# A two-expert mixture layer: every expert on every token, or each expert on its own gathered tokens

## The chip, the core and the metric

The kernel runs on one core of a Trainium2 chip. The metric is the device time of one execution in microseconds (us). The engines are PE (matrix multiply; PEld is its weight load), DVE (vector), ACT (activation), POOL (GpSimd) and SP, which here only issues DMAs. PSUM is the memory that PE writes; it has eight banks of 128 x 512 floats.

## The reference, cut to what matters

x has 4096 tokens (2 x 2048) of 256 features. The same mixture-of-experts layer (MoE) runs twice, before and after a full attention; an LSTM layer, a causal attention and a second LSTM follow, and the change touches none of them.

```
x = x + 0.5 * ffn(layernorm(x))
x = x + attention(layernorm(x))
x = x + 0.5 * ffn(layernorm(x))
...
def ffn(x):
    probs = sigmoid(xt @ gate_w.T + gate_b)          # 6 experts
    w, idx = top_k(probs, 2)
    w = w / (sum(w) + 1e-08)
    ge = sum(one_hot(idx, 6) * w[..., None])         # 0 but for two experts of a token
    for e in range(6):
        h = silu(xt @ ew1[e].T) * (xt @ ew3[e].T)
        y = y + ge[:, e:e + 1] * (h @ ew2[e].T)
    z = silu(xt @ fc1.T) * (xt @ fc2.T) @ fc3.T      # shared expert, every token
    return y + z
```

All matrices are 256 x 256. A token has weight 0 for four of its six experts.

## The kernel before, in words

x stays in SBUF as `k.X` (128 partitions x 32 tiles of 128 tokens). `program` runs the stages one after another; between two stages all engines meet. `moe_stage` is the first and the third stage.

It works on 8 blocks of 512 tokens (`NBLK`), and in each block on 7 experts: the six and the shared one. Every product of floats is split in a high and a low part (`x_hi`, `x_lo`, `w_hi`, `w_lo`), and three products stand for one, so the first layer of one expert on one block (`up`) is 2 halves of 12 matmuls with 512 columns, and the second layer (`down`) is 24 matmuls with 256 columns. An **expert block** below is one `up` and one `down`. There are 8 x 7 = 56 of them in a stage.

All seven experts' split weights stay in SBUF; they are split once, in the first block (`split`, ACT at L377 and DVE at L484).

For each half of `up`, ACT takes the sigmoid (L395), DVE multiplies twice (L449, L453), ACT rounds the result to the high part (L387) and POOL makes the low part (`blockwise` of POOL, L274). `down` waits for it. DVE then adds the block's output, times the token's weight for that expert, into x (`update`, L465).

The routing of block n+1 is put between the experts of block n: DVE's layer norm (L107 to L120, L133, with one POOL step at L126), PE's transposes (L142), ACT's and DVE's split of x (L363, L473), PE's gate (L292, eight matmuls of 512 columns), a sigmoid, a transpose back (L299), and DVE's choice of two experts (`gate`, L422 to L441). The order on each engine is the order in which the code is written, and semaphores tie the engines together. SP loads weights only. POOL issues no DMA in this stage; it issues some in the causal attention (L1606, L1615).

## Time and profile before

| | us |
|---|---|
| median of 3 runs | 4684.81 (4669.04 to 4697.14) |
| the profiled execution | 4671.09 |
| its span, first to last instruction | 4669.5 |
| PE busy in it | 4239.2 (91%) |
| DVE busy | 3004.6 (64%) |
| ACT busy | 2295.4 (49%) |
| POOL busy | 682.8 (15%) |

A busy PE is one that has a matmul in flight; matmuls overlap, so the mean duration of one is longer than the distance between two starts. The two MoE stages lie at about 16 to 542 us and 2178 to 2699 us.

### The profile page before, as it was taken

The numbers are of one execution on the slowest core, as the hardware profiler recorded it, in microseconds if no ns is written. First come the engines' busy times: TensorE is split into PE (matmuls) and PEld (weight loads), VectorE is DVE, ScalarE is ACT, GpSimd is POOL, SyncE is SP. The second block draws the span as 40 slices with busy tenths as digits, with TensorE's granted clock in tenths as the row PEclk, the third lists the DMA queues.
The fourth block names the chain that finished last, engine by engine and source line by source line (L and its number), as shares of the span: only waits on it lengthen the run. The fifth ranks groups of instructions, "written<-read, shape, count | busy, mean of one in ns | idle before, by whom it ended". The sixth has DMA issues, their size and how long they took to land. (4 is left out here: it accounts for less than half of the span.)

```text
span 4669.5 us, 79371 instructions
## 1 busy us (share of the span) xinstructions
PE 4239.2 (91%) x25648; PEld 2522.6 (54%) x25648; DVE 3004.6 (64%) x5513; ACT 2295.4 (49%) x4375; POOL 682.8 (15%) x698
## 2 busy tenths in 40 slices
PE   7999969999999999986999989639999999997688
PEld 6888743333333333324888855525656656654454
DVE  5556668888888888835656533746666666663432
ACT  3222317777777777761332222214656556655222
POOL 2232200000000000000233200532222222220000
PEclk9999979999999999987999999868999989998789
DMA  2000172323323322203000000476667667662401
GB/s 85 0 0 0 52 146 38 46 34 43 46 34 44 46 38 39 32 6 120 8 0 0 1 20 0 150 198 179 188 176 184 188 165 186 191 158 52 131 20 36
DMA packets 173944, 359.15 MB, mean 77 GB/s; under 512 B 40586, under 2 KB 104714, under 8 KB 156810
## 3 DMA queue, kind: packets, MB, share of 16 engines
q1 hardware_dynamic: 154634, 304.20, 28.5%
q0 software_dynamic: 18944, 50.35, 3.9%
q8 instruction: 196, 3.21, 0.3%
q14 instruction: 170, 1.39, 0.1%
HBM read 209.71 MB, written 152.06 MB: 77 GB/s over the span
## 5 line engine op out<-in xcount | busy, mean ns | idle before, releaser
L1314 DVE TENSOR_REDUCE full_tops<-psum 128x1 f32<-128x1024 f32 x1024 | 1206.2, 1218 | 184.0 <-PE psum L1218 184.0
L1271 ACT ACTIVATE full_probs<-psum 128x512 f32<-128x512 f32 x2048 | 1065.8, 602 | 299.2 <-PE psum L1190 295.1
L1781 ACT ACTIVATE causal_probs<-psum 128x512 f32<-128x512 f32 (+3 forms) x1280 | 640.2, 533 | 397.9 <-PE psum L1653 230.0
L1190 PE MATMUL psum<-full_q,full_k 49*128 49x512 f32 x2048 | 653.3, 475 | 23.2 <-ACT full_probs L1271 17.2
L1832 DVE TENSOR_REDUCE causal_tops<-psum 128x1 f32<-128x1024 f32 (+7 forms) x704 | 586.8, 857 | 112.6 <-PE psum L1704 112.6
L1190 PEld LDWEIGHTS psum<-full_q,full_k 49*128 49x128 f32 x2048 | 284.5, 186 | 605.8 <-ACT full_probs L1271 576.9
L1199 PE MATMUL psum<-full_probs,full_vh 128*32 128x512 f32 x4096 | 556.8, 616 | 0.7 <-ACT full_probs L1271 0.7
L1218 PE MATMUL psum<-full_k,full_q 48*128 48x512 f32 x2048 | 402.0, 458 | 51.4 <-DMA full_k<-qk_split 23.6
L1653 PE MATMUL psum<-causal_q,causal_k 49*128 49x512 f32 (+3 forms) x1280 | 407.7, 451 | 14.2 <-ACT causal_probs L1781 8.3
L1704 PE MATMUL psum<-causal_k,causal_q 48*128 48x512 f32 (+4 forms) x1152 | 325.3, 414 | 70.2 <-DVE causal_tops L1847 33.4
L274 POOL TENSOR_TENSOR moe_h_lo<-moe_h,moe_h_hi 128x512 fp32r<-128x512 f32 x224 | 290.3, 1296 | 661.2 <-ACT moe_h_hi L387 661.2
L311 PE MATMUL psum<-moe_x_hi,moe_w_hi 128*128 128x512 f32 x896 | 351.9, 393 | 4.3 <-DVE moe_h L453 4.1
L311 PE MATMUL psum<-moe_x_lo,moe_w_hi 128*128 128x512 f32 x896 | 349.9, 391 | 0.0
L311 PE MATMUL psum<-moe_x_hi,moe_w_lo 128*128 128x512 f32 x896 | 348.8, 389 | 0.0
L1683 PE MATMUL psum<-causal_probs,causal_vh 128*32 128x384 f32 (+3 forms) x3712 | 343.0, 433 | 1.2 <-ACT causal_probs L1781 1.2
L449 DVE TENSOR_TENSOR moe_ts<-psum,moe_sg 128x512 f32<-128x512 f32 x224 | 154.7, 691 | 294.3 <-ACT moe_sg L395 294.1
L387 ACT CAST moe_h_hi<-moe_h 128x512 fp32r<-128x512 f32 x224 | 139.0, 620 | 384.7 <-DVE moe_h L453 384.7
L1606 POOL DMA_DIRECT2D band_scores<-xn x256 | 188.0, 734 | 841.8 <-DVE causal_tops L1847 838.1
L1218 PEld LDWEIGHTS psum<-full_k,full_q 48*128 48x128 f32 x2048 | 198.3, 190 | 207.5 <-DVE full_tops L1314 157.7
L1847 DVE CUSTOM_DVE_ANT_0 xn<-psum,causal_bias 128x160 f32<-128x160 f32 (+1 forms) x512 | 143.4, 317 | 202.0 <-issue 202.0
L395 ACT ACTIVATE moe_sg<-psum 128x512 f32<-128x512 f32 x224 | 133.9, 598 | 257.9 <-PE psum L311 256.6
L325 PE MATMUL psum<-moe_w_hi,moe_h_hi 128*128 128x256 f32 x896 | 255.9, 286 | 2.5 <-POOL moe_h_lo L274 2.5
(190 smaller groups left out, 6070.7 us busy)
## 6 DMA issues: line engine op xcount, KB each, us to landing
causal_bias<-bias_tiles SPq DMA_DIRECT2D x32, 1280.0 KB, 6.3
band_scores<-xn POOLq DMA_DIRECT2D x256, 160.0 KB, 4.2
full_q<-qk_split SPq DMA_DIRECT2D x192, 128.0 KB, 6.3
full_k<-qk_split SPq DMA_DIRECT2D x192, 128.0 KB, 7.1
causal_q<-rot_parts SPq DMA_DIRECT2D x192, 128.0 KB, 5.4
causal_k<-rot_parts SPq DMA_DIRECT2D x192, 128.0 KB, 6.4
bias_tiles<-causal_skew_rows SPq DMA_DIRECT2D x32, 640.5 KB, 3.4
bias_tiles<-causal_skew_rows SPq DMA_DIRECT2D x32, 640.0 KB, 3.3
```

The source lines that it names most:

```text
L274: nc.gpsimd.tensor_tensor(h_lo[:, r, u % C, :], hf[:, u % 2, :], h[:, r, u % C, :].bitcast(F32), ALU.subtract).then_inc(hl_ready, 1)
L311: last = nc.tensor.matmul(k.psum[:, 2 * (u % 2) + kind, :], W[wp][:, e, kind, c, m * P:(m + 1) * P], (xhi, xlo)[xp][:, half, c, :], start= ...
L1190: nc.tensor.matmul(k.psum[:, b, :], k_sb[at, q, kt * P:(kt + 1) * P], q_sb[at, q, n * BLK:(n + 1) * BLK], start=True, stop=True).then_inc( ...
L1199: last = nc.tensor.matmul(k.psum[32 * j:32 * j + VP, 7, :], vh[:, q % 2, kt, :], pT[:, kt % 4, j * BLK:(j + 1) * BLK], start=(kt == 0), st ...
L1218: last = nc.tensor.matmul(k.psum[:, b + c, :], q_sb[at, q, t * P:(t + 1) * P], k_sb[at, q, lo:lo + BLK], start=True, stop=True)
L1271: nc.scalar.activation(pT[:, kt % 4, n * BLK:(n + 1) * BLK], k.psum[:, bank(q, u), :], ACT.Exp).then_inc(p_ready, 1)
L1314: nc.vector.reduce_max(mx[:, q % 2, u // 2, u % 2:u % 2 + 1], src, AX_X).then_inc(m_free, 1)
L1653: last = nc.tensor.matmul(k.psum[:, b, 0:(hi - lo) * P], k_sb[at, q, kt * P:(kt + 1) * P], q_sb[at, q, lo * P:hi * P], start=True, stop=no ...
L1683: last = nc.tensor.matmul(k.psum[32 * j:32 * j + VP, 7, tiles[0] // QB * P:BLK], vh[:, q % 2, kt, :], pT[:, n % 2, first:first + QB * (len ...
L1704: last = nc.tensor.matmul(k.psum[:, b + side, at0:at0 + hi - lo], q_sb[at, q, t * P:(t + 1) * P], k_sb[at, q, lo:hi], start=True, stop=True)
L1781: nc.scalar.activation(dst, k.psum[:, bank(q, u), 0:(hi - lo) * P], ACT.Exp).then_inc(p_ready, 1)
L1832: last = nc.vector.reduce_max(mx[:, r, t, entry:entry + 1], both[:, off:off + hi - lo], AX_X)
```

## The change

`moe_stage` is rewritten; a token now meets the shared expert and its two experts only. In four phases:

1. **Shared expert with the routing.** For each of 8 blocks the shared expert runs (8 expert blocks), and the routing goes on: `choose` and `weigh` as before, then `positions` on PE (six small matmuls with a triangle and with ones) counts for each token and expert how many tokens came before it, `locate` on DVE turns that into a slot number in a list of its expert, and POOL writes the token's number to the two slots with indirect DMAs of 128 x 4 bytes (`scatter`, 8 a block, 64 in all). SP stores the normalised rows to DRAM (`XN`).
2. **Plan.** `schedule` on DVE works out which expert each of 21 blocks belongs to and where its list lies.
3. **21 expert blocks** of 512 list places each. SP loads the block's token numbers, POOL gathers the rows with four indirect DMAs of 128 rows of 1 KB (`gather`), PE transposes them, ACT and DVE split x and also the weights of the block's expert (`split`, `rest`, in a ring of three), `up` and `down` run as before, ACT copies the output (`out`) and SP stores it. 8192 pairs of token and expert fill at least 16 blocks, and six lists round up to at most 21; 21 are always run.
4. **Combine.** After all stores, POOL gathers for each of the 32 tiles of x its two output rows (64 indirect DMAs of 128 x 1 KB), and DVE adds them with their weights.

So there are 8 + 21 = 29 expert blocks in a stage in place of 56. The code is written out, without loops. The heart of the diff:

```diff
-                looped(pool, NBLK, blockwise)
+                def scatter(n):
+                    pool.wait_ge(idx_ready, n + 1)
+                    for t in range(n * TB, (n + 1) * TB):
+                        for s in range(2):
+                            pool.indirect_dma_start(
+                                out=k.TOKENS[:, :], out_offset=bass.IndirectOffsetOnAxis(ap=idx[:, s, t:t + 1], axis=0),
+                                in_=token[:, t:t + 1], in_offset=None).then_inc(k.scattered, 16)
+                def gather(b):
+                    v = NBLK + b
+                    pool.wait_ge(s_id[b % 4], 16 * (b // 4 + 1))
+                    pool.wait_ge(t_ready, 2 * (v - 2) + 2)
...
+                    for t in range(TB):
+                        pool.indirect_dma_start(
+                            out=k.xn[:, v % 2, t, :], out_offset=None, in_=k.XN[:, :],
+                            in_offset=bass.IndirectOffsetOnAxis(ap=idr[:, b % 4, t:t + 1], axis=0)).then_inc(k.gathered[v % 2], 16)
...
+                for v in range(NBLK - 2):
+                    rest(v + 1, 0)
+                    rest(v + 1, 1)
+                    scatter(v + 2)
+                    if v + 4 < NBLK:
+                        ln.pool_rstd(pool, v + 4, v % 2)
...
+                for v in range(NBLK, NV - 1):
+                    rest(v + 1, 0)
+                    if v + 3 < NV:
+                        gather(v + 3 - NBLK)
+                    rest(v + 1, 1)
+                for r in range(2):
+                    pool.wait_ge(s_y[r], 16 * ((NX + 1 - r) // 2))
+                pool.wait_ge(back_ready, 1)
+                for g in range(TT):
+                    if g >= 8:
+                        pool.wait_ge(c_done, g - 7)
+                    for s, ring in enumerate((k.xn, ybuf)):
+                        pool.indirect_dma_start(
+                            out=ring[:, g % 8 // TB, g % TB, :], out_offset=None, in_=k.YS[:, :],
+                            in_offset=bass.IndirectOffsetOnAxis(ap=back[:, s, g:g + 1], axis=0)).then_inc(k.back[g % 8], 16)
```

PE, phases 1 and 3 (`up(v, m)` is one half, `down(v, pair)` too):

```diff
-                    for e in range(E + 1):
-                        if e < E:
-                            up(n, half, e + 1)
...
-                        down(n, half, e)
+                transpose(0)
+                gate(0)
+                positions(0)
+                transpose(1)
+                gate(1)
+                positions(1)
+                up(0, 0)
+                up(0, 1)
+                for v in range(NBLK - 2):
+                    transpose(v + 2)
+                    up(v + 1, 0)
+                    gate(v + 2)
+                    up(v + 1, 1)
+                    down(v, 0)
+                    positions(v + 2)
+                    down(v, 1)
...
+                transpose(NBLK)
+                transpose(NBLK + 1)
+                up(NBLK, 0)
+                up(NBLK, 1)
+                for v in range(NBLK, NV):
+                    if v + 1 < NV:
+                        up(v + 1, 0)
+                    if v + 2 < NV:
+                        transpose(v + 2)
+                    if v + 1 < NV:
+                        up(v + 1, 1)
+                    down(v, 0)
+                    down(v, 1)
```

The new gate has the tokens as the stationary side, so its result needs no transpose back: for each of four tiles one matmul for the bias and four for x, of six columns each. ACT and DVE:

```diff
+            # ACT, phase 3
+                for v in range(NBLK, NV):
+                    if v + 1 < NV:
+                        hidden(v + 1, 0)
+                    if v + 2 < NV:
+                        upper_x(v + 2)
+                    if v + 1 < NV:
+                        hidden(v + 1, 1)
+                    out(v - NBLK, 0)
+                    out(v - NBLK, 1)
+                    if v + 3 < NV:
+                        split(v + 3 - NBLK)
+            # DVE, phase 1
+                for v in range(NBLK - 2):
+                    lower_x(v + 2)
+                    hidden(v + 1, 0)
+                    choose(v + 2)
+                    hidden(v + 1, 1)
+                    weigh(v + 2)
+                    update(v)
+                    locate(v + 2)
+                    if v + 3 < NBLK:
+                        apply(v + 3)
+                    if v + 4 < NBLK:
+                        ln.dve_stats(dve, v + 4, v % 2, (v + 4) * TB)
+            # DVE, phase 4
+                for g in range(TT):
+                    dve.wait_ge(k.back[g % 8], brought(g))
+                    xt = k.X[:, g, :]
+                    nc.vector.scalar_tensor_tensor(xt, k.xn[:, g % 8 // TB, g % TB, :], wgt[:, 0, g:g + 1], xt,
+                                                   ALU.mult, ALU.add).then_inc(c_half, 1)
+                    dve.wait_ge(c_half, g + 1)
+                    nc.vector.scalar_tensor_tensor(xt, ybuf[:, g % 8 // TB, g % TB, :], wgt[:, 1, g:g + 1], xt,
+                                                   ALU.mult, ALU.add).then_inc(c_done, 1)
```

`hidden(v, m)` is the sigmoid, the two products and the rounding of one half; `rest(v, m)` on POOL is the old L274; `split` and `rest` of the weights read the block's expert from the plan with a register load first.

**POOL in the loop over the 21 blocks.** Before, POOL's queue in a MoE stage held the low part of each half and the layer norm's step:

```order
L265 MEMSET moe_pT 128x1024
L126 ISA
L126 TENSOR_TENSOR lnv<-lnv,neghalf 128x4
L149 UNCONDITIONAL_BRANCH
L149 ISA
L274 TENSOR_TENSOR moe_h_lo<-moe_h,moe_h_hi 128x512
```

Now, around the change from phase 1 to phase 3 (`normed` is `XN`, `slot_tokens` the lists):

```order
L376 DMA slot_tokens<-moe_token,moe_idx 24576x1 x8
L395 TENSOR_TENSOR moe_h_lo<-moe_h,moe_h_hi 128x512 x2
L388 DMA xn<-normed,moe_ids 128x256 x8
L395 TENSOR_TENSOR moe_h_lo<-moe_h,moe_h_hi 128x512
L388 DMA xn<-normed,moe_ids 128x256 x4
L395 TENSOR_TENSOR moe_h_lo<-moe_h,moe_h_hi 128x512 x2
L388 DMA xn<-normed,moe_ids 128x256 x4
```

A block's four gathers stand between the low parts of two halves, and the gather of a block stands behind the low part of the block two before it.

**DVE at the end of an iteration of phase 1**, with its waits: what stands behind the wait for `down` (the update, L758), up to the rows that the next transposes need (L133):

```order
L758 SCALAR_TENSOR_TENSOR X<-psum,X 128x512 [waits moe0_dn_ready] x2
L673 TENSOR_TENSOR moe_slot<-psum,moe_tables 128x24 [waits moe0_pos_ready]
L676 TENSOR_TENSOR moe_slot<-moe_slot,moe_sel 128x24 [waits moe0_pos_free]
L678 TENSOR_REDUCE moe_hi_slot<-moe_slot 128x4 [waits moe0_l_dve]
L679 TENSOR_REDUCE moe_both<-moe_slot 128x4
L681 TENSOR_TENSOR moe_lo_slot<-moe_both,moe_hi_slot 128x4 [waits moe0_l_dve]
...
L693 TENSOR_REDUCE moe_wgt<-moe_top_w 128x4 [waits moe0_wgt_ready]
L694 TENSOR_REDUCE moe_wgt<-moe_is_low 128x4
L133 TENSOR_SCALAR xn<-X,lnv 128x256 [waits moe0_ln_rstd,moe0_xn_stored1,moe0_t_ready]
L133 TENSOR_SCALAR xn<-X,lnv 128x256 x3
```

Before, the layer norm of the next block stood among the experts of a block, five expert blocks ahead of the `up` that reads it; now it stands behind the wait for the last `down` of the iteration, and PE's next instruction after that `down` is the transpose that needs it.

## Rows read from the trace of the kernel before

**Rows 1.** The page: busy tenths of PE in 40 slices of the span.

```profile
PE   7999969999999999986999989639999999997688
```

**Rows 2.** Windows: PE, PEld, DVE, ACT, POOL busy (count), clock, DMA share, GB/s.

```profile
110.00:170.00 60.00, 60.00 (x337) 50.41 (x336) 35.50 (x70) 18.70 (x32) 18.32 (x15) 1.00 0.01 1
```

**Rows 3.** Timeline of PE, start and duration in us: one expert block.

```profile
290.43 0.28 PE L325 MATMUL psum<-moe_w_hi,moe_h_hi 128*128 128x256 f32 x1
...
293.30 0.40 PE L311 MATMUL psum<-moe_x_hi,moe_w_hi 128*128 128x512 f32 x1
...
298.77 0.28 PE L325 MATMUL psum<-moe_w_hi,moe_h_hi 128*128 128x256 f32 x1
```

**Rows 4.** Timeline: the first MoE stage's start, its first up, its end.

```profile
16.21 0.95 POOL L265 MEMSET moe_pT<- 128x1024 f32 x1 [15.51 <-POOLq L49]
...
32.87 0.47 PE L311 MATMUL psum<-moe_x_hi,moe_w_hi 128*128 128x512 f32 x1
...
541.54 0.76 DVE L465 SCALAR_TENSOR_TENSOR X<-psum,X 128x256 f32<-128x256 f32 x2 [0.68 <-PE psum L325]
```

**Rows 5.** The two lines whose DMAs POOL issues: min/median/max ns, landing.

```profile
L1606 POOL DMA_DIRECT2D band_scores<-xn x256: 725/725/902, 3121.7 to 4248.0; - x128
...
DMA to landing us min/median/max: 2.3/4.2/11.7
...
L1615 POOL DMA_DIRECT2D band_compact<-band_scores x32: 1117/1136/1145, 3169.3 to 4251.2; - x32
...
DMA to landing us min/median/max: 4.2/5.4/10.6
```

**Rows 6.** Groups by shape, 37 to 542 us: busy us, mean ns, idle before.

```profile
L274 POOL TENSOR_TENSOR moe_h_lo<-moe_h,moe_h_hi 128x512 fp32r<-128x512 f32 x112 | 145.2, 1296 | 330.6 <-ACT moe_h_hi L387 330.6
...
L449 DVE TENSOR_TENSOR moe_ts<-psum,moe_sg 128x512 f32<-128x512 f32 x112 | 77.3, 690 | 147.0 <-ACT moe_sg L395 146.8
L387 ACT CAST moe_h_hi<-moe_h 128x512 fp32r<-128x512 f32 x112 | 69.5, 621 | 194.3 <-DVE moe_h L453 194.3
...
L465 DVE SCALAR_TENSOR_TENSOR X<-psum,moe_ge,X 128x256 f32 x96 | 40.8, 475 | 18.2 <-PE psum L325 18.0
...
L473 DVE TENSOR_TENSOR moe_x_lo<-psum,moe_x_hi 128x512 fp32r<-128x512 f32 x14 | 8.9, 679 | 0.0
...
L377 ACT CAST moe_w_hi<-moe_w_in 128x1536 fp32r<-128x1536 f32 x4 | 5.9, 1482 | 0.0
```

**Rows 7.** The split of the weights on DVE: min/median/max ns.

```profile
L484 DVE TENSOR_TENSOR moe_w_lo<-moe_w_in,moe_w_hi x14: 1742/1759/2174, 26.5 to 2236.2; 128x1536 fp32r<-128x1536 f32 x14
```

**Rows 8.** Timeline of DVE: layer norm, and the first and last routing operation.

```profile
16.62 1.41 DVE L107 BATCH_NORM_STATS2 st<-X 128x6 f32<-128x256 f32 x4 [15.49 <-PEq L49]
...
20.05 1.38 DVE L133 TENSOR_SCALAR xn<-X,lnv 128x256 f32<-128x256 f32 x4 [1.13 <-POOL lnv L126]
...
33.43 0.31 DVE L422 TENSOR_TENSOR moe_gt<-moe_pr 128x144 f32<-128x144 f32 x1 [5.19 <-ACT moe_pr L367]
...
35.86 0.18 DVE L441 SCALAR_TENSOR_TENSOR moe_ge<-moe_wsel,moe_tot 128x24 f32<-128x24 f32 x1
```

**Rows 9.** Timeline of PE: transposes and small products.

```profile
21.54 1.94 PE L142 MATMUL psum<-ident_sb,xn 128*128 128x128 f32 x8 [21.54 <-DVE xn L133]
...
94.22 0.60 PE L299 MATMUL psum<-ident_sb,moe_pT 128*128 128x128 f32 x4
...
2708.03 5.28 PE L2311 MATMUL psum<-big,arena 128*128 128x1 f32 x24 [9.65 <-DMA big<-in_bo]
```

**Rows 10.** DMA issues: count, KB each, median us to landing.

```profile
qk_split<-qkvf_parts SPq DMA_DIRECT2D x32, 512.0 KB, 4.2
...
full_q<-full_rows SPq DMA_DIRECT2D x64, 8.0 KB, 1.9
```

**Rows 11.** Windows at the start of the second MoE stage, columns as above.

```profile
2182.00:2193.00 11.00, 8.45 (x20) 2.87 (x21) 3.32 (x4) 4.51 (x5) 0.00 (x0) 0.60 0.47 172
2193.00:2197.00 4.00, 4.00 (x21) 3.33 (x20) 3.14 (x11) 3.43 (x4) 0.00 (x0) 1.00 0.01 4
```

More of the change, by code:

```diff
@@ new lines, in moe_stage @@
+        more = sb("more", [P, E, NBLK])
+        nblk = sb("nblk", [P, E])
+        prior = sb("prior", [P, E, E])
+        first = sb("first", [P, E])
+        total = sb("total", [P, 1])
+        past = sb("past", [P, NX, E - 1])
+        base = sb("base", [P, NX, E - 1])
+        expert = sb("expert", [P, NX])
+        valid = sb("valid", [P, NX])
+        origin = sb("origin", [P, NX])
+        inner = sb("inner", [P, NX])
+        row = sb("row", [P, NX])
+        plan = sb("plan", [P, 2, NX], I32)
@@ new lines, in gate @@
+                def gate(n):
+                    pe.wait_ge(xl_ready, 2 * n + 2)
+                    for t in range(TB):
+                        out = k.psum[:, 6, t * E:(t + 1) * E]
+                        nc.tensor.matmul(out, one_row[:, :], gb[:, :], start=True, stop=False, skip_group_check=True)
+                        for x, half in enumerate((xhi, xlo)):
+                            for c in range(C):
+                                last = nc.tensor.matmul(out, half[:, n % 3, c, t * P:(t + 1) * P].bitcast(F32), gwT[:, c, :],
+                                                        start=False, stop=(x == 1 and c == C - 1), skip_group_check=True)
+                    last.then_inc(gate_ready, 1)
@@ new lines, in _ @@
+                up(NBLK - 1, 0)
+                up(NBLK - 1, 1)
+                for v in (NBLK - 2, NBLK - 1):
+                    down(v, 0)
[11 more added lines that the diff above has]
+                        up(v + 1, 1)
+                    down(v, 0)
+                    down(v, 1)
```

671 lines of the change are left out of this document (446 added, 225 removed).

## The prediction

> **What bounds the kernel now.** I read the page first. PE's busy line has two stretches of nines, slices 0 to 4 and 18 to 23 [rows 1]; these hold the two MoE stages. A window inside one shows PE busy for 60.00 of 60 us at the full granted clock (1.00, that is 2.4 GHz), while DVE has 35.5, ACT 18.7 and POOL 18.3 us [rows 2]. So PE sets the pace. The timeline gives its price: one `down` takes from 290.43 to 293.30, 2.87 us, and one `up` from there to 298.77, 5.47 us; an expert block is **8.34 us** [rows 3]. 56 of them are 467 of the 526 us of the stage, which runs from 16.2 to 542.3 us [rows 4]; the rest is start, transposes and gates. Nothing POOL does bounds this stage. The change takes away 27 expert blocks, 225 us of PE a stage, and puts in their place work that waits on POOL and on DMAs. I walk through the first stage on its own clock and take the same saving for the second.
>
> **Up to the first `up`.** Now it starts at 32.87 us [rows 4]. PE's new order has two whole routings ahead of it. Block 0's gate should end about where it does now, at 31.8. It is 20 small matmuls in place of 8 wide ones. The trace does not show this shape; the nearest rows are 24 products of one column in 5.28 us, 0.22 each, and 4 transposes in 0.60 us once PE is warm, about 0.12 each [rows 9]. So a gate costs 4.4 us cold and 2.4 warm, and 8 transposes 1.94 cold, 1.0 warm. DVE's small operations run at (36.04 - 33.43) / 10 = 0.26 us where each waits for the last [rows 8]; some of the new ones don't, so I take 0.23. `choose`, `weigh` and `locate` have 7 + 6 + 13 = 26 of them, 6.0 us. After 31.8: sigmoid and these 26, to 38; block 1's rows 1.4 and the next layer norm 2.7 [rows 8], to 42; low part of x 1.4 [rows 6], gate 4.4, choice and count 3. **First `up` at 51 us**, 18 later than now. A clock still at its low level there would cost up to 5 more: at the start of the second stage the granted clock is 0.60, about the 1.2 GHz level for most of the window, and 1.00 from 2193 on [rows 11].
>
> **Phase 1, six iterations.** PE has per block 8.34 + 1.0 + 2.4 + 0.7 = 12.4 us, but it waits. Followed round the loop from the transposes: DVE's layer norm 2.65, low part of x 1.36 [rows 6, 8], gate 2.4, half an `up` 2.7, sigmoid and two products 2.0, `weigh` 1.4; `down` is over by then; update 1.4, `locate` 2.9, normalised rows 1.4, and only then the next transposes. That is **18 us** an iteration, 5.5 of it PE idle behind `update`, `locate` and `apply`. The first ends at 76.5, since POOL puts 16 scatters ahead of its first low part; then four of 18, and 16.7 without the last `apply`: 165 us.
>
> **The price that decides: g**, POOL's time to issue one indirect DMA of 128 rows. The trace has none. Its two direct ones take 0.725 us and 1.136 us [rows 5]; the second has an irregular pattern. An indirect one must also fetch and use 128 separate numbers, so I take the dearer row, **g = 1.13**; below it the bound is 0.73, above it I allow 2.0, some 0.9 more than any row, since no row excludes it. Landing L after the issue: the shortest and the median landing of line L1606 are 2.3 and 4.2 us from the start of the issue [rows 5], so 1.6 to 3.5; I take 2.5, as SP's 512 KB stores run beside the gathers. The Trainium skill ("DMA: Bandwidth & Descriptors", Anatomy of one DMA) gives about 2.0 us and the bytes at 436 GB/s for a DMA from POOL; for 128 KB that is 2.3 us in all, an estimate of L = 1.2, by which the sum would be some 34 us lower over both stages. The trace's shortest landing agrees with it, its median does not.
>
> **From phase 1 to phase 3.** The last list numbers are ready at about 164.5. Then, in a row: 8 scatters 9.0, landing 2.5, a register load and the ids 3 (8 KB land in 1.9 [rows 10]), 8 gathers 9.0 because PE transposes two blocks before the first `up`, landing 2.5, transposes 1: **192 us**. The last two `down` and the plan (11 small operations, 2.8 us, and two splits) lie beside it.
>
> **Phase 3.** PE needs 1.0 + 8.34 = 9.34 us a block. ACT has 1.24 x 2 for the halves, 1.2 for x and 1.2 for the output (all at the 0.62 of the rounding), and 1.48 for the weights: 6.4. DVE has 2.8 + 1.36 + 1.76: 5.9 [rows 6, 7]. POOL has 2 x 1.3 + 4g = 7.1. None of these sums bounds. The chain does: from the end of the first half of one `up`: sigmoid, products and rounding 2.65, low part 1.3, four gathers 4.52, landing 2.5: 11.0 us, against 9.34 until PE reaches these transposes. A late transpose delays the next `up` but not the gather issued after the half before it, so only half of the difference is paid: a block takes 9.34 + (11.0 - 9.34) / 2 = **10.15 us**. The register loads on ACT and DVE have no row; hidden in the slack of both I take nothing, up to 10 us a stage. Sum: one `up` 5.5, 20 x 10.15, one `down` 2.9: 403 us. Copy and store 4.8 [rows 10]: **408 us**.
>
> **Combine.** All stores must land first, so nothing hides this. 64 x 1.13 = 72.3 us of issues; DVE needs 2 x 0.475 a tile [rows 6], less than two issues, so it follows. The last landing and two additions take 3.6: the stage ends at **484 us**, against 542.3. That saves **58 a stage, 116 in all**. The next stages start as now.
>
> **The sum** against the profiled execution: 4671.1 - 116 = 4555 us. That execution was 14 us below the median; against the median it is 4684.8 - 116 = **4569 us**.
>
> How it depends on g: entry to phase 3 has 16, phase 3 has 20 x 4 / 2 = 40 and the combine 64, so each us of g costs 120 us a stage. The gain of 58 is used up at **g = 1.61**.
>
> **Rivals.**
>
> *The issue is dear (the other side).* At g = 2.0 the entry grows 14 us, phase 1 about 10 (POOL then has 8 x 2.0 + 1 + 2.6 = 19.6 us a block, over the 18), phase 3 35 and the combine 56: 115 a stage, 4799 us. It decides from g = 1.61 on. For it: no row shows an indirect DMA, and this one has one number for each row, where a direct one has a stride. Against it: the irregular direct DMA costs only 0.4 more than the plain one. Chance 0.25.
>
> *The issue is cheap.* At g = 0.73 phase 3 falls to PE's 9.34 (16 less), the entry by 6, the combine by 26: 48 a stage, 4473 us. For it: 0.725 is by far the most frequent row. Against it: those DMAs have no list. Chance 0.12.
>
> *PE at the low clock in phase 1.* If waits of 5 us in every iteration keep the granted clock near 0.60 [rows 11], matmuls of 12.4 us take up to 10 more, seven times, and the start 5: up to 75 a stage, of which waits hide a third: 50. 4569 + 100 = 4669, no change. Against it: now the clock is 1.00 through the stage, though PE there never waits so regularly. Chance 0.08.
>
> *DVE and POOL in each other's way.* The split of weights reads two tiles in SBUF; it took 1.74 to 2.17 us [rows 7]. If each such operation holds POOL up whole, the combine has 64 x 0.475 = 30 and phase 3 has 21 x 1.76 / 2 = 18: 48 a stage, 4665 us, no change. The row's spread of 0.4 bounds what has been seen. The Trainium skill ("SBUF — State Buffer", Who interferes with whom) says that a DVE instruction with two SBUF inputs contends with a GpSimd instruction that reads SBUF; all of the combine's additions are such, and by that rule it would come out this way; no row settles whether a DMA issue counts as such an instruction. Chance 0.05.
>
> That the change does not do less work can be excluded: 29 expert blocks are written out, whatever the data.
>
> **Numbers.** Forecast 0.50, dear 0.25, cheap 0.12, clock 0.08, contention 0.05. A measurement of this kernel tells about 0.5%, 23 us, from no change; that is 0.1 in g. Forecast and cheap give faster, 0.62. Clock and contention count half as the same, and a slice of the dear case near g = 1.6 too: same 0.09. Dear, and the clock or contention on top of a somewhat dearer issue: slower 0.29. The range runs from the cheap case to the dear one, each cut slightly: 4480 to 4790.
>
> **What would show it.** In the profile after: POOL's DMA lines show g, best in the combine, where starts should be 1.13 apart and the stretch about 75 us long. The starts of the first halves in phase 3 should be 10.15 apart, with PE waiting for the gathers' DMAs. In phase 1 they should be 18 apart, with PE waiting for DVE's normalised rows, at clock 1.00. The first stage should end at 484 us, and the other stages should keep their lengths. The forecast is wrong if g is over 1.6, if 8.34 grows, or if another wait than the gather's sets phase 3.

## The result: 3.4% slower, where 2.5% faster was forecast

The changed kernel takes 4843.91 us (median, 4835.12 to 4853.72), the kernel before beside it 4690.98 (4669.04 to 4706.23). The ratio is **1.034**, 95% interval 1.030 to 1.038. The forecast was 4569 us, its range ended at 4790, and its break-even for g, POOL's price of an indirect DMA, was 1.61 us. The profiled execution took 4853.7 us, span 4852.2. The first stage ends at 619.2 us, against 542.3 before [rows 4] and 484 in the forecast; the second one is as much longer (77.6 us from its first transposes to its last addition). Twice 77 is 154; the difference of the medians is 153. Each stage missed its forecast by 135 us.

The page of the changed kernel, beside the slices shown of before [rows 1]:

```profile
PE   6868368999999999995878729666999999998688
...
PEclk8789687999999999976679859885999999999799
```

The nines of PE in the MoE stages (now slices 0 to 5 and 18 to 23) are gone, and the granted clock there is mostly 0.6 to 0.8. The windows of the first stage tell its parts apart:

```profile
core 0: us, PE busy (x) PEld busy (x) DVE busy (x) ACT busy (x) POOL busy (x), PEclk, DMA share, GB/s
...
80.00:110.00 30.00, 26.26 (x119) 23.09 (x120) 14.41 (x56) 3.99 (x8) 11.38 (x11) 0.67 0.08 18
...
140.00:180.00 40.00, 32.52 (x159) 28.89 (x158) 22.31 (x89) 6.18 (x11) 17.38 (x17) 0.71 0.13 27
...
220.00:275.00 55.00, 26.34 (x138) 23.62 (x137) 19.18 (x52) 10.31 (x13) 20.05 (x19) 0.70 0.20 20
...
330.00:500.00 170.00, 138.93 (x752) 120.40 (x751) 76.43 (x94) 77.36 (x122) 86.69 (x82) 0.91 0.28 87
...
540.00:620.00 80.00, 0.00 (x0) 0.00 (x0) 31.03 (x64) 0.00 (x0) 57.79 (x62) 0.50 0.35 102
```

Phase 1 (80 to 220) has PE busy for 0.8 to 0.9 of the time, but at a clock of about 0.7. The transition (220 to 275) has it busy for half. In phase 3 (330 to 500) it is busy for 82%. In the combine it does nothing for 80 us.

**The price g was right.** The source view of POOL's three indirect lines:

```profile
L376 POOL DMA_INDIRECT slot_tokens<-moe_token,moe_idx x128: 954/958/1896, 42.7 to 2490.5; - x128
```

```profile
L388 POOL DMA_INDIRECT xn<-normed,moe_ids x168: 942/946/1002, 256.0 to 2755.7; - x168
```

```profile
L432 POOL DMA_INDIRECT moe_y<-slot_outputs,moe_back x64: 942/946/948, 537.9 to 2864.6; - x64
```

0.946 us busy and 0.30 us between two make 1.25 from start to start; 1.13 was forecast. The combine ran from 536.6 to 619.2, 82.6 us where 75.9 was forecast. So neither rival about g holds, and the loss is elsewhere. That the number was near is in part luck: the forecast took the dearer row because 128 numbers must be fetched, and e6 below shows the same price for 64.

**Phase 1.** DVE's update of block v starts at 89.08, 115.98, 143.09, 170.30: **27.2 us** an iteration, where 18 was forecast. PE's timeline through a part of one:

```profile
148.42 1.97 PE L142 MATMUL psum<-ident_sb,xn 128*128 128x128 f32 x8 [3.74 <-DVE xn L133]
150.04 0.77 PE L484 MATMUL psum<-moe_x_hi,moe_w_hi 128*128 128x512 f32 x1
150.61 0.63 PE L484 MATMUL psum<-moe_x_lo,moe_w_hi 128*128 128x512 f32 x1
151.04 0.63 PE L484 MATMUL psum<-moe_x_hi,moe_w_lo 128*128 128x512 f32 x1
...
154.39 0.40 PE L484 MATMUL psum<-moe_x_lo,moe_w_hi 128*128 128x512 f32 x1
154.63 0.40 PE L484 MATMUL psum<-moe_x_hi,moe_w_lo 128*128 128x512 f32 x1
154.96 0.38 PE L454 MATMUL psum<-moe_gb,moe_one_row 1*128 1x6 f32 x2
155.27 0.61 PE L457 MATMUL psum<-moe_gwT,moe_x_hi 128*128 128x6 f32 x4
...
157.96 1.02 PE L457 MATMUL psum<-moe_gwT,moe_x_hi 128*128 128x6 f32 x4
...
162.01 0.77 PE L484 MATMUL psum<-moe_x_hi,moe_w_hi 128*128 128x512 f32 x1
...
167.92 0.31 PE L502 MATMUL psum<-moe_w_hi,moe_h_hi 128*128 128x256 f32 x1
```

The starts of the wide matmuls are 0.43 apart at 150.6 and 0.24 from 154.4 on, so the clock is at its low level (1.2 GHz) after the wait of 3.74 us, and comes back. It falls a second time inside the gate: four records of L457 take 0.61 at 155.27 and 1.02 at 157.96. It comes back only at 168. PE waits 3.74 us in an iteration, less than the 5.5 that were forecast, so its own work takes 23.5 us in place of 12.4. The gate itself is 40 records, two for each of 20 matmuls: 7.0 us here, 9.35 at the stage's start (26.3 to 35.6).

**The transition.** The timeline of all engines and of POOL, from the last scatter to the first gather:

```profile
236.88 1.76 DVE L768 TENSOR_TENSOR moe_w_lo<-moe_w_raw,moe_w_hi 128x1536 fp32r<-128x1536 f32 x1 [3.59 <-issue]
237.57 1.90 POOL L376 DMA_INDIRECT slot_tokens<-moe_token,moe_idx  x1 [0.30 <-issue]
...
254.05 3.73 SPq L350 DMA_DIRECT2D moe_ids<-slot_tokens  x4
...
255.98 1.00 POOL L388 DMA_INDIRECT xn<-normed,moe_ids  x1 [13.99 <-DMA moe_ids<-slot_tokens]
```

SP's load of the token numbers starts 16.5 us after the last scatter starts (12.3 in the second stage), where the forecast had 2.5 for the landing and 3 for register load and ids together.

**Phase 3** takes 12.4 us a block (the gathers' groups start at 304.18 and, 16 blocks later, at 502.69), where 10.15 was forecast. PE's waits from 262 to 530:

```profile
PE psum L142 <- DMA xn<-normed,moe_ids: 66.3, 13, 17.3
```

One of the 13 waits is the first, 17.3 us; the other twelve are 49 us, about 4.1 in every second block.

### The profile page after: what moved, and what is told of

Read it like the earlier page. It is cut to its first block and busy times, and to the rows that moved or that the text cites. A ratio compares the mean times of both kernels' runs of the same rounds, so it can differ in the third digit from the quotient of the medians.

```text
span 4852.2 us, 75781 instructions
## 1 busy us (share of the span) xinstructions
PE 4054.0 (84%) x24032; PEld 2387.4 (49%) x24032; DVE 2879.4 (59%) x5431; ACT 2283.3 (47%) x4341; POOL 942.0 (19%) x1014
## 5 line engine op out<-in xcount | busy, mean ns | idle before, releaser
L1526 PE MATMUL psum<-full_q,full_k 49*128 49x512 f32 x2048 | 661.5, 482 | 20.3 <-ACT full_probs L1607 13.4
L1535 PE MATMUL psum<-full_probs,full_vh 128*32 128x512 f32 x4096 | 567.0, 627 | 0.7 <-ACT full_probs L1607 0.7
L1989 PE MATMUL psum<-causal_q,causal_k 49*128 49x512 f32 (+3 forms) x1280 | 412.0, 456 | 14.6 <-ACT causal_probs L2117 8.3
L142 PE MATMUL psum<-ident_sb,xn 128*128 128x128 f32 x720 | 133.6, 347 | 310.0 <-DVE xn L133 174.6
L1508 POOL COPY full_vh<-full_values 128x256 f32 (+1 forms) x32 | 12.8, 400 | 1349.6 <-PE psum L1535 1347.3
L142 PEld LDWEIGHTS psum<-ident_sb,xn 128*128 128x128 f32 x720 | 110.1, 180 | 332.7 <-DVE xn L133 177.8
L2000 PE MATMUL psum<-ident_sb,causal_bias 128*128 128x128 f32 x1024 | 258.2, 335 | 0.0
L1989 PEld LDWEIGHTS psum<-causal_q,causal_k 49*128 49x128 f32 x1280 | 175.9, 190 | 125.0 <-issue 78.9
L2040 PEld LDWEIGHTS psum<-causal_k,causal_q 48*128 48x128 f32 x1152 | 186.4, 198 | 87.1 <-DVE causal_tops L2183 37.8
L484 PE MATMUL psum<-moe_x_hi,moe_w_hi 128*128 128x512 f32 x464 | 222.8, 480 | 0.4 <-issue 0.4
L395 POOL TENSOR_TENSOR moe_h_lo<-moe_h,moe_h_hi 128x512 fp32r<-128x512 f32 x116 | 148.6, 1284 | 373.3 <-ACT moe_h_hi L564 366.6
```

Of the source, the lines that this page charges most:

```text
L142: last = nc.tensor.transpose(k.psum[:, bank, t * P:(t + 1) * P], k.xn[:, half, t, c * P:(c + 1) * P], k.ident[:, :])
L1526: nc.tensor.matmul(k.psum[:, b, :], k_sb[at, q, kt * P:(kt + 1) * P], q_sb[at, q, n * BLK:(n + 1) * BLK], start=True, stop=True).then_inc( ...
L1535: last = nc.tensor.matmul(k.psum[32 * j:32 * j + VP, 7, :], vh[:, q % 2, kt, :], pT[:, kt % 4, j * BLK:(j + 1) * BLK], start=(kt == 0), st ...
L1989: last = nc.tensor.matmul(k.psum[:, b, 0:(hi - lo) * P], k_sb[at, q, kt * P:(kt + 1) * P], q_sb[at, q, lo * P:hi * P], start=True, stop=no ...
L2000: last = nc.tensor.matmul(k.psum[:, b, at:at + P], bt[:, q, t, REL:BAND], k.ident[:, :], start=False, stop=True, skip_group_check=True)
L2040: last = nc.tensor.matmul(k.psum[:, b + side, at0:at0 + hi - lo], q_sb[at, q, t * P:(t + 1) * P], k_sb[at, q, lo:hi], start=True, stop=True)
```

## The experiments

There are thirteen kernels. "Stage" is the first MoE stage, and its end is 619.2 us in the changed kernel; the second behaved alike unless the text says otherwise. A ratio is to the kernel before; a time without a ratio is that of a single execution. An iteration is one of the six steps of phase 1's loop, and "locate" marks its end. The cuts of the code are against the changed kernel where nothing else is said.

### e1: DVE's order in phase 1

```diff
                     hidden(v + 1, 1)
+                    if v + 3 < NBLK:
+                        apply(v + 3)
                     weigh(v + 2)
+                    locate(v + 2)
                     update(v)
-                    locate(v + 2)
-                    if v + 3 < NBLK:
-                        apply(v + 3)
```

> Only DVE's order in phase 1 changes: the normalised rows of block v+3 and locate(v+2) come ahead of update(v). Theory A (the chain: PE's transposes wait behind update, locate and apply on DVE, and the matmuls are slow because of nothing else): the 4 to 5 us of PE idle before each transpose go, the iteration falls from 27.2 to about 22.5 us, the granted clock stays near 0.70, a stage is about 28 us shorter. Theory B (the idle lowers the clock and the clock makes most of the iteration): the clock goes back to 1.00 and the iteration falls to 16 to 18 us, a stage is 50 to 60 us shorter. If neither holds (the rows of XN or POOL hold the loop), it stays at 27.

4801.22 us, ratio 1.025 (1.022 to 1.029). An iteration takes about 24.4 us, the stage ends at 599.5, 19.7 earlier, and the clock between 110 and 140 is 0.83. So neither theory holds as written: the idle before the transposes went (1.2 us are left), but the gate still ran at the low clock, and now stood behind a wait of 2.36 us for x_lo.

### e2: extra matmuls where PE waits

```diff
                     down(v, 1)
+                    if v + 3 < NBLK:
+                        fill(v + 2)
```

`fill` is 16 matmuls of 512 columns into bank 6, which the transposes overwrite.

> 16 extra matmuls of 512 columns, into a bank that nobody reads, stand in PE's queue where it waits for the next normalised rows in phase 1; the chain of waits is as in the changed kernel. Theory A (chain): 27.2 us an iteration stays or grows by 1 to 3 us. Theory B (clock): the granted clock in 100:200 rises from 0.70 to 0.9 or more and the iteration falls to 19 to 21 us although PE does 3.7 us more work.

4795.6 us. The iteration is 22.2 us, clock 0.84 to 0.89, stage end 593.3: **5 us an iteration less with 3.8 us more work**. This is close to theory B, whose upper end was 21 us. So the low clock is a cause in itself. The chain of waits of DVE is as it was. PE is now busy all the time, and yet the clock still falls once an iteration. The end of the gate and what follows, in PE's timeline:

```profile
142.65 0.38 PE L454 MATMUL psum<-moe_gb,moe_one_row 1*128 1x6 f32 x2
...
147.32 0.59 PE L457 MATMUL psum<-moe_gwT,moe_x_lo 128*128 128x6 f32 x4
147.77 0.71 PE L484 MATMUL psum<-moe_x_hi,moe_w_hi 128*128 128x512 f32 x1
148.27 0.63 PE L484 MATMUL psum<-moe_x_lo,moe_w_hi 128*128 128x512 f32 x1
...
151.50 0.39 PE L484 MATMUL psum<-moe_x_hi,moe_w_hi 128*128 128x512 f32 x1
```

This gate ran at the full clock and took 5.1 us, from 142.65 to the next half at 147.77, where 2.4 were forecast. So part of the gate's cost is its own work, and part is the clock.

### e3: a gate of 8 matmuls

```diff
-                        nc.tensor.matmul(out, one_row[:, :], gb[:, :], start=True, stop=False, skip_group_check=True)
-                        for x, half in enumerate((xhi, xlo)):
+                        for x, half in enumerate((xhi,)):
...
```

> Leaves out the gate's bias products and its products with the low part of x, so the gate is 8 matmuls a block in place of 20 (routing probabilities differ slightly). If the gate's price is that of its number of passes (0.233 us each at the low clock, two for each matmul): a gate falls from 9.35 to 3.7 us at the start, the first half of an up comes at 50 in place of 61 us, and the iteration falls by up to 5.6 us, to 21.6. If the gate in the loop is hidden by the wait on DVE: the iteration stays at 27.

4773.53 us. The first half of an `up` starts at 49.5 us, as the first theory had it (50), and the first gate takes 3.55 us in place of 9.35: there its price goes by the number of records. The steps from one locate to the next, from the third on, are 29.9, 19.2, 29.6, 17.6 and 18.7 us, 23.0 in the mean; stage end 593.0. The gate is then 1.84 us for 16 records, 0.115 each, where it runs at the full clock. The two long steps hold a standstill that the profile names no engine and no DMA for. In the first one all engines stand; DVE's timeline has:

```profile
115.72 0.69 DVE L757 SCALAR_TENSOR_TENSOR X<-psum,X 128x512 f32<-128x512 f32 x1 [11.02 <-remote]
```

The second one has 8.66 us of the same kind on ACT. What they are stays open; e13 has one too. In the second stage, where none falls into them, the same five steps take 19.9 us in the mean, 7.3 below the changed kernel, where the records alone were to give 5.6.

### e4: POOL gathers first

```diff
                 for v in range(NBLK, NV - 1):
-                    rest(v + 1, 0)
                     if v + 3 < NV:
                         gather(v + 3 - NBLK)
+                    rest(v + 1, 0)
                     rest(v + 1, 1)
```

SP's stores move one step back as well, so that the token numbers come in time.

> In phase 3 POOL issues the gathers of block v+3 ahead of the low part of the half of block v+1, as soon as the transposes of v+1 have left the buffer, and SP loads the token numbers one block further ahead of the stores. If the gather behind the low part of the half is what holds phase 3 (period 12.4 us, PE waiting 4.1 us in every second block): period 9.4 to 10 us, no PE wait for xn, a stage about 50 us shorter, the whole about 100 us. If the cause is another one (the weights' split with its register load, DVE or ACT): the period stays above 11.5.

4773.18 us, ratio 1.020 (1.014 to 1.026). PE no longer waits for a gather in the loop, the clock from 330 to 500 is 0.99, and the stage ends at 580.6, 38.6 earlier (36.4 of it behind the first gather). But a block takes 10.9 us, not 9.4. Three engines in one block, from the timeline:

```profile
375.14 1.48 ACT L573 CAST moe_w_hi<-moe_w_raw 128x1536 fp32r x1
...
377.65 1.76 DVE L768 TENSOR_TENSOR moe_w_lo<-moe_w_raw,moe_w_hi 128x1536 fp32r<-128x1536 f32 x1 [4.03 <-issue]
...
378.35 1.88 POOL L388 DMA_INDIRECT xn<-normed,moe_ids  x1 [0.30 <-issue]
...
379.33 0.69 DVE L746 TENSOR_TENSOR moe_ts<-psum,moe_sg 128x512 f32<-128x512 f32 x1
...
381.91 1.29 DVE L628 TENSOR_TENSOR moe_x_lo<-psum,moe_x_hi 128x512 fp32r<-128x512 f32 x2 [1.17 <-ACT moe_x_hi L550]
...
383.31 0.47 PE L484 MATMUL psum<-moe_x_hi,moe_w_hi 128*128 128x512 f32 x1 [1.41 <-issue]
```

DVE waits for ACT's split of the weights (its end 376.62), then 1.03 us for its register load, splits, and only then, at 379.33, takes the half that PE had finished before 376. The low part of x comes late, and PE waits 1.41 us for it.

### e5: the last block's scatters left out

```diff
-                    scatter(v + 2)
+                    if v + 3 < NBLK:
+                        scatter(v + 2)
```

SP's count of awaited scatters is lower by these eight.

> Leaves out the 8 scatters of the last block (its tokens reach no expert list), and SP waits for the others alone. Between the last scatter and the first gather lie 18.4 us in the changed kernel, 14.3 in its second stage. If that is the landing of the scatters (4-byte writes): with their landing long past, the first gather comes 5 to 8 us after the last locate, where it now comes 27.7 after it. If it is what SP does then (its register load and the 2 KB load of token numbers): at least 14 us after the last locate stay.

4835.6 us. SP's load of the token numbers in its timeline:

```profile
228.23 3.73 SPq L350 DMA_DIRECT2D moe_ids<-slot_tokens  x4
```

It starts 1.0 us after the plan is ready (227.2); in the changed kernel it was 22.1 (from 231.97 to 254.05). So the register load is cheap and **the wait is for the scatters**. The first gather comes 13.7 us after the last locate (223.68 to 237.34), between the two expectations. The rest is POOL: it stands behind the low part of the last half, which waits for DVE, which splits weights first.

### e6: what an issue is paid for

```diff
-                            out=ring[:, g % 8 // TB, g % TB, :], out_offset=None, in_=k.YS[:, :],
+                        out=k.xn[0:P // 2, g % 8 // TB, g % TB, :], out_offset=None, in_=k.YS[:, :],
...
+                    pool.dma_start(ybuf[:, g % 8 // TB, g % TB, :], k.YS[g * P:(g + 1) * P, :]).then_inc(k.back[g % 8], 16)
```

> In the combine each indirect gather of 128 rows for the first expert becomes one of 64 rows, and each one for the second a direct DMA of 128 KB from POOL (the sums are then not the layer's). If the 0.946 us of an issue is paid per row named: the 64-row ones take 0.5 to 0.6 us and the direct ones 0.73 (the row of the kernel before). If it is a fixed price of the indirect form: 64 rows stay at 0.9 to 0.95, direct ones 0.73. The 0.30 between two issues stays in either case; the combine then takes 32 x (0.95 + 0.73 + 0.6) = 73 us or 32 x (0.55 + 0.73 + 0.6) = 60, against 80.

4798.27 us. POOL's timeline in the combine:

```profile
559.05 0.97 POOL L431 DMA_INDIRECT xn<-slot_outputs,moe_back  x1 [0.30 <-issue]
560.03 0.59 POOL L434 DMA_DIRECT2D moe_y<-slot_outputs  x1
560.92 0.94 POOL L431 DMA_INDIRECT xn<-slot_outputs,moe_back  x1 [0.30 <-issue]
```

With 64 rows named in place of 128 an issue still takes 0.95 (median of 64): between 64 and 128 rows **the price goes by the form and not by the rows**. A direct one takes 0.59, not the 0.73 expected, and the 0.30 stands ahead of the indirect one alone. A pair takes 1.87, and the combine 62 us (538.6 to 600.6), where 73 was expected for a fixed price.

### e7: e1, e4 and the weights' split later

```diff
                     if v + 2 < NV:
                         upper_x(v + 2)
+                    if NBLK < v and v + 2 < NV:
+                        split(v + 2 - NBLK)
                     if v + 1 < NV:
                         hidden(v + 1, 1)
...
-                    if v + 3 < NV:
-                        split(v + 3 - NBLK)
```

DVE's `rest` of the same weights follows `hidden(v + 1, 1)`.

> The orders of the two runs before that changed DVE in phase 1 and POOL in phase 3, and a third: in phase 3 ACT's and DVE's splits of the weights stand one step later, behind the next block's x. Theory: what was left at 10.9 us a block in phase 3 is the chain output, weight split, register load, low part of the weights, next half, on ACT and DVE; with it gone PE sets 9.4 us and phase 3 takes 198 us. Then the stage ends at 619 - 16 - 63 = 535 to 545 us, the whole at 4680 to 4700, level with the kernel before. Rival: ACT or DVE is full (6.4 and 5.9 us of work and two register loads): the period stays at 10.9 and the whole at 4730.

4827.38 us, ratio 1.031 (1.027 to 1.034): a miss on both sides. The period rose from 10.9 to 13.5 us in most blocks. The waits from 330 to 480 say why:

```profile
PE psum L484 <- DVE moe_w_lo L768: 26.1, 11, 2.4
```

The weights now came just before their `up`, behind the half they should have let pass. I had moved the pair of steps past its due time.

### e8: the gate mixed into the half

On top of e7: ten gate records behind every three matmuls of the second half of `up`, and DVE's statistics and rows while they run.

```diff
-                    gate(v + 2)
-                    up(v + 1, 1)
+                    gate_in_up(v + 2, v + 1)
```

> As the run before, and in phase 1 the gate's 40 narrow passes stand in four groups between the matmuls of the second half of the up, and DVE takes the next block's statistics and rows while they run. Theory (the gate, 5 to 9 us of matmuls of 6 columns with a wait ahead of it, is what lowers the clock in phase 1): the clock in 100:200 is at 0.95 or more, an iteration takes 16 to 18 us in place of 24.5, a stage another 40 to 50 us less, the whole 4580 to 4620 us, faster than the kernel before. Rival (the idle alone does it): the clock stays near 0.8 and the iteration above 21 us.

4823.43 us, ratio 1.030 (1.025 to 1.034). Theory and rival both fall. The window is the clearest row of the study:

```profile
140.00:180.00 40.00, 40.00 (x177) 35.59 (x177) 22.66 (x90) 4.89 (x10) 16.44 (x17) 0.60 0.22 27
```

**PE is busy for 40.00 of 40 us and has a clock of 0.60.** By this profile it never waits (busy means that a matmul is in flight), so idle time is not needed for the low clock. What keeps it low is settled by e9 and e10, which differ in the gate alone. An iteration takes 21 to 24 us of nothing but PE work.

### e9: all orders, with the weights' low part in its place

As e8 but with the gate in one piece, ACT's split where the change had it, and in DVE's phase 3:

```diff
                         hidden(v + 1, 0)
+                    if NBLK < v and v + 2 < NV:
+                        rest(v + 3 - NBLK)
                     if v + 2 < NV:
                         lower_x(v + 2)
                     if v + 1 < NV:
                         hidden(v + 1, 1)
-                    if v + 3 < NV:
-                        rest(v + 4 - NBLK)
```

Its register load also stands ahead of its wait.

> Gate narrow and in one piece, as in the changed kernel. Phase 1: DVE takes statistics and rows of the next block while the gate runs, and locate ahead of update. Phase 3: gathers first, ACT's split of the weights where the changed kernel has it, but DVE's half of it moved behind the next step's first half instead of ahead of it, with its register load ahead of its wait. Theory for phase 3 (the 10.9 us were output, weight split, register load and low part of the weights ahead of the next half; the 13.5 of the three orders came from putting both parts too late): 9.4 to 9.6 us a block, PE-bound, clock 1.00; rival (DVE or ACT full): 10.9 stays. Phase 1: 21 to 24.5 us an iteration, clock 0.6 to 0.85. The whole 4690 to 4730 us.

4642.65 us, ratio **0.987** (0.981 to 0.994): 1.3% faster than the kernel before, and below what was expected. The gathers' groups are 9.30 us apart, and PE is full. Two windows, one of phase 1, whose last locate is at 189.7, and one of phase 3:

```profile
100.00:175.00 75.00, 74.80 (x393) 67.19 (x394) 51.54 (x180) 13.57 (x26) 39.47 (x39) 0.75 0.19 29
...
275.00:330.00 55.00, 55.00 (x335) 48.88 (x334) 33.10 (x42) 32.67 (x53) 41.83 (x36) 1.00 0.38 113
```

Phase 1 takes 20.7 us an iteration, with PE busy for 74.80 of 75 us and the clock at 0.75: again no idle, again a low clock. PE's timeline shows it fall:

```profile
135.19 0.39 PE L484 MATMUL psum<-moe_x_hi,moe_w_lo 128*128 128x512 f32 x1
...
137.28 0.61 PE L457 MATMUL psum<-moe_gwT,moe_x_hi 128*128 128x6 f32 x4
...
139.04 1.02 PE L457 MATMUL psum<-moe_gwT,moe_x_hi 128*128 128x6 f32 x4
```

Wide matmuls have run without a wait since 132.57, 0.23 apart, which is the full clock. The clock falls inside the gate, at about 138, while PE is busy, and comes back at about 148, at the end of the wide matmuls behind it.

### e10: e9 with the wide gate of the kernel before

```diff
+                                last = nc.tensor.matmul(k.psum[0:E, 6, :], gwT[:, c, :], half[:, n % 3, c, :].bitcast(F32),
+                                                        start=(x == 0 and c == 0), stop=(x == 1 and c == C - 1))
...
+                def turn(n):
+                    pe.wait_ge(odds_ready, n + 1)
+                    for t in range(TB):
+                        last = nc.tensor.transpose(k.psum[:, 6, t * P:(t + 1) * P], pT[:, n % 2, t * P:(t + 1) * P], k.ident[:, :])
```

> As the run before, with the gate of the kernel before put back: 4 matmuls of 512 columns in place of 20 of 6, a sigmoid on 6 rows, four transposes back in the middle of the next half, a copy. Theory (narrow matmuls lower the clock, busy or not): the clock in 100:200 goes to 0.95 or more, an iteration takes 15.5 to 18 us, a stage is 30 to 45 us shorter than in the run before, the whole 4610 to 4650 us, below the kernel before. Rival (the chain through the gate sets the iteration at any clock): 21 us or more stay, and the whole stays above 4690.

4599.77 us, ratio **0.979** (0.974 to 0.985). The stage ends at 500.5, 15.7 earlier than in e9. The window of phase 1 has the clock at 0.92 although PE is busy for only 88% there:

```profile
100.00:175.00 75.00, 66.23 (x325) 48.28 (x325) 53.23 (x182) 17.57 (x32) 43.36 (x43) 0.92 0.15 22
```

This is the clean comparison: nothing but the gate differs, and the version that waits more has the higher clock, 0.92 for 0.75. The two gates differ in the columns that move (6 or 512) and in what is stationary; no run tells these apart. The whole is a little below the 4610 to 4650 expected, but clock, iteration and stage fall short of the theory. At 19.6 us an iteration PE's work fell, and a wait became the bound. DVE and PE in the timeline:

```profile
131.64 2.22 DVE L133 TENSOR_SCALAR xn<-X,lnv 128x256 f32<-128x256 f32 x4 [4.65 <-POOL lnv L126]
...
135.59 0.41 PE L472 MATMUL psum<-moe_held,moe_ones 128*128 128x30 f32 x2 [3.92 <-DVE moe_sel L662]
```

POOL's step of the layer norm stood behind eight scatters, DVE waited for it, and PE for DVE.

### e11: the wide gate alone

The changed kernel with the gate of e10 and nothing else.

> The changed kernel with nothing but its gate undone (the wide form). Theory (two causes of the low clock in phase 1: the narrow gate, and PE idle 3.7 us ahead of the transposes): the idle remains, so the clock still falls once an iteration but not twice: 0.8 to 0.9 in 100:200, and 21 to 24 us an iteration in place of 27.2. If the gate is the only cause: clock 0.95 and 19 to 20 us. If the idle is the only one: clock 0.70 and 26 us.

4737.41 us. The clock from 100 to 175 is 0.91, against 0.70 in the changed kernel, and an iteration takes 20.3 us; the stage ends at 570.5. **One undone edit gives 6.9 us of the 9.2 that phase 1 missed per iteration**, and 48.7 us of a stage with the shorter start. It lands between the first two expectations, at the lower end in time. The gate in PE's timeline, behind the same wait of 3.74 us:

```profile
142.40 1.10 PE L142 MATMUL psum<-ident_sb,xn 128*128 128x128 f32 x8 [3.74 <-DVE xn L133]
...
147.77 1.88 PE L457 MATMUL psum<-moe_x_hi,moe_gwT 128*6 128x512 f32 x4
149.49 1.88 PE L457 MATMUL psum<-moe_x_lo,moe_gwT 128*6 128x512 f32 x4
151.30 0.50 PE L492 MATMUL psum<-moe_x_hi,moe_w_hi 128*128 128x512 f32 x1
```

Not all of the 6.9 us is the clock. At the full clock the narrow gate takes 5.1 us (e2), the wide one 3.5 (147.77 to 151.30) and its transposes back some 0.4; by this estimate 1.2 us are the gate's own work and 5.7 the clock.

### e12: half the scatters

```diff
-                        for s in range(2):
+                        for s in range(1, 2):
```

> The changed kernel with only the scatters of each token's second list number (4 a block in place of 8), so half of the list places stay zero. In the changed kernel SP's first load of token numbers starts 14.6 us after the end of the last scatter's issue begins (237.57 to 254.05 is 16.5 from its start; 12.3 in the second stage). If the landing is a backlog (each 128 single writes of 4 bytes take longer than the 1.25 us between two issues): with half of them 7 to 9 us from the last scatter's start. If it is a fixed delay of such a write: 15 to 17 us stay, and the first gather comes only 5 us earlier, by the four issues.

4861.46 us. SP's load in its timeline, with the last scatter's start at 233.67:

```profile
248.31 3.73 SPq L350 DMA_DIRECT2D moe_ids<-slot_tokens  x4
```

14.6 us from start to start (15.0 in the second stage), against 16.5 and 12.3 with twice the scatters. So it is **not a backlog**: half as many scatters do not shorten the wait. The packets of the scatters are in the trace until about 244 us in the changed kernel; what fills the ten us from there to 254 it does not show.

### e13: choose ahead of the rows

Against e10:

```diff
+                    choose(v + 2)
                     if v + 3 < NBLK:
                         apply(v + 3)
-                    choose(v + 2)
                     hidden(v + 1, 1)
```

> As the run with the wide gate, but in phase 1 DVE's choose stands ahead of the next block's rows. There DVE waited 4.65 us for POOL's step of the layer norm, which stands in POOL's queue behind eight scatters, and PE waited 3.92 us for the choice behind it. Theory (this wait, made by the price of the scatters, is what is left of phase 1 over PE's own work): the iteration falls from 19.6 to 15.7 to 17 us, the clock in 100:200 rises from 0.89 to 0.95 or more, a stage is 16 to 24 us shorter, the whole 4550 to 4575 us. Rival (another wait takes its place, the rows themselves): 18.5 us or more stay and the whole at 4585 or more.

4590.73 us, ratio **0.978** (0.976 to 0.981), the same as e10 within the intervals. The clock from 100 to 175 is 0.95, as expected. Four of five steps between locates are 16.6 to 18.1 us, a little over what was expected, and the fifth is 25.8: ACT stood still, again without a releaser in the profile, in its timeline:

```profile
111.10 0.60 ACT L575 ACTIVATE moe_sg<-psum 128x512 f32<-128x512 f32 x1 [12.16 <-remote]
```

So the wait named was real, but the first stage of this execution won nothing by it: its five steps take 96 us in both versions, and it ended at 501.8. In the second stage, which has no such standstill, the same five steps take 89.2 us against 95.8 in e10.

## Why the prediction was wrong

- **g and the combine: right, g in part by luck.** It is 1.25 from start to start for 1.13, which adds about 7 us in the combine; the reason given for 1.13, the 128 numbers, is not what is paid for (e6). The case that was to end on the other side (dear issue, chance 0.25) did not happen; the kernel is slower for other reasons.
- **The saving on PE: right in kind.** 29 expert blocks run, and where nothing else binds one costs 9.30 us with its transposes (e9), 9.34 forecast.
- **First `up` at 51 us: it came at 61.** The term that failed is the gate, priced as 20 small matmuls from a row that named 24 records [rows 9]. These were two records for each of 12 matmuls, so a matmul costs some 0.47 at the low clock and not 0.22: two gates at 9.35 in place of 4.4 account for the 10 us.
- **Phase 1, 18 us an iteration "at clock 1.00": 27.2.** This is the step that failed most, +53 us. The wait was not what was wrong: PE waits 3.74 us an iteration, where 5.5 were forecast. Its own work takes 23.5 us in place of 12.4. Some 3.3 us of the difference are small matmuls that were priced too low (the gate 5.1 at the full clock for 2.4, `positions` 1.3 for 0.7); the other 7.8 are the low clock, by this estimate. It stood among the rivals (PE at the low clock, chance 0.08), and its 50 us a stage lie near the 53 by luck, since it had the low clock come from the waits alone. What I missed is that the change brings its own cause. Undoing the narrow gate gives 6.9 us an iteration (e11). The clock falls inside it with PE busy (e9) and is higher with the wide gate, although PE then waits (e10). The idle behind update, locate and apply is a second cause: filling it raises the clock (e2), and behind that wait the clock falls in e11 too. The Trainium skill ("TensorE: Matmul & The Clock Gate", HAM oscillation — how this bites in real kernels) puts such low clocks down to waits between groups of matmuls; e2 and e11 agree in part, the windows of e8 (40.00 of 40 us busy at 0.60) and e9 show it without a wait.
- **Entry to phase 3: +17 us.** "Landing 2.5" was taken from L1606, DMAs of 160 KB. From the start of the last scatter to the first gather 18.4 us pass, where 6.6 were forecast: SP's load starts only 12 to 16.5 us after that scatter, whether 8 or 4 such DMAs stand before it (e12). The Trainium skill ("DMA: Bandwidth & Descriptors", Anatomy of one DMA) has about 2 us fixed for a DMA from POOL; the gathers agree roughly (in the combine the rows are used 2.8 us after the start of the last issue, 615.43 to 618.22), the scatters do not.
- **Phase 3, 10.15 us a block: 12.4, +48 us.** The chain behind the first half was the right one, and e4 took it out: 36 us. But "only half of the difference is paid" was a guess, and the split of the weights with its register loads was the next bound at 10.9. The split stood in the sums of ACT and DVE alone and the loads were taken as "hidden in the slack of both"; neither stood in the chain. e9 moved that one step and reached 9.30. Slack in sums of busy time (6.4 and 5.9 of 9.34 us) did not hide a step that stood at the wrong place of a queue.
- **DVE and POOL in each other's way (0.05): seen, but not where it was priced.** Beside the split of the weights an issue takes 1.9 us in place of 0.95 (the scatter at 237.57, the gather at 378.35 in e4). In the combine 64 additions with two SBUF inputs leave the issues at 0.942 to 0.983. The Trainium skill ("SBUF — State Buffer", Who interferes with whom) has a DVE instruction with two SBUF inputs contend with a GpSimd instruction that reads SBUF. If an issue counts as one, the first operation fits and the second does not, and no run tells why they differ; the rival's 30 us in the combine did not come.
- **The other stages kept their lengths** within the spread: together they are 28 us longer in the profiled execution, which lies 10 above its median, while that of before lies 20 below its own.

The errors add up: +10, +53, +17, +48 and +7 are 135 us a stage. All have the same sign, since most came from a cost set to zero or to a row that was too cheap; the one wait that was priced too high, PE's in phase 1, is small beside them.

## What to carry to other kernels

Taking work from a full engine pays only if the order of every queue still feeds it: the kernel with the same 29 blocks a stage ran in 4844 us and, with four steps moved and the gate put back, in 4600. Put a dependent step (here a gather, here the weights' low part) where its input is surely ready and its user still a full step away, and check both sides; e7 shows the cost of one step too late. Count the records of a matmul against the code before taking a price from them, and ask of each new small matmul what clock its neighbours will run at.

## What the runs showed that I had not expected

- 40 records of 6 columns in each block kept PE's granted clock at 0.60 to 0.75 with no idle time (e8, e9); with 4 matmuls of 512 columns in their place it was 0.92 with PE idle for 12% of the time (e10).
- 16 matmuls that compute nothing made an iteration 5 us shorter (e2).
- An indirect DMA costs POOL the same 0.95 us for 64 rows as for 128, and 0.30 more ahead of it; a direct one 0.59 (e6).
- 4-byte scatters are waited for 12 to 16.5 us after the last issue starts, with 8 or with 4 of them in the last block (e12); without them the load starts at once (e5).
- Standstills without a releaser, which made a step 8 to 11 us longer, occurred in two of the versions (e3, e13). Their cause is open.
